# First projections and table products of the self attention issued in the last step of the cross attention, and the first step's queries rotated by VectorE

## The reference, cut to what matters

```python
x = x + tanh(g_xattn[0]) * _L0_xattn_ref(_layernorm(x), ctx_2048, ...)
x = x + tanh(g_ffn[0]) * _L0_ffn_ref(_layernorm(x), ...)
...
# inside _L0_ffn_ref: _attention(_layernorm(hidden_states, ln1_w, ln1_b), ...)
q = (h @ wq + bq); k = (h @ wk + bk); v = (h @ wv + bv)
q = q * cos + _rotate_half(q) * sin
k = k * cos + _rotate_half(k) * sin
scores = einsum('bhqd,bhkd->bhqk', q, k) / sqrt(HD)      # causal softmax
out = einsum('bhqk,bhkd->bhqd', probs, v) @ wo + bo
```

## Time and profile before

| what | value |
|---|---|
| median of 3 runs | 1759.58 us (1757.66 to 1762.4) |
| profiled execution, its own time | 1763.62 us |
| its span | 1761.7 us |
| mean granted TensorE clock | 0.978 |
| TensorE matmuls busy | 1665.8 us (95%) |
| VectorE busy | 1179.1 us (67%) |
| ScalarE busy | 1304.5 us (74%) |
| GpSimd busy | 1133.9 us (64%) |

### The profile page before, as it was taken

The page is one execution under the profiler, slowest core; times in us unless marked ns, Lnnn a source line. Parts: engine busy times, 40 slices in busy tenths (PEclk is TensorE's granted clock), DMA queues, the critical chain, the costliest instruction groups (busy, mean ns, idle before and its releaser), DMA issues.

```text
span 1761.7 us, 35497 instructions
## 1 busy us (share of the span) xinstructions
PE 1665.8 (95%) x11136; PEld 1513.4 (86%) x11136; DVE 1179.1 (67%) x3193; ACT 1304.5 (74%) x4205; POOL 1133.9 (64%) x1293
## 2 busy tenths in 40 slices
PE   6899998799999999999997996999999999999898
PEld 3788887688999999999996885899999999988897
DVE  5567668577775666566776787777777777776322
ACT  5677777598888888887874554898898988988321
POOL 5455536899998989898962214565655656676454
PEclk8899999899999999999998999999999999999998
DMA  4111211100000000000002010000000000000000
GB/s 148 51 40 36 67 32 55 43 19 13 19 19 13 15 24 13 20 13 20 13 7 93 23 30 8 13 9 12 10 12 13 9 13 16 17 15 15 10 19 25
DMA packets 32841, 45.87 MB, mean 26 GB/s; under 512 B 5264, under 2 KB 21904, under 8 KB 32656
## 3 DMA queue, kind: packets, MB, share of 16 engines
q1 hardware_dynamic: 32656, 43.59, 8.2%
HBM read 39.39 MB, written 4.19 MB: 25 GB/s over the span
## 4 chain that ended last, share of the span: by engine, by line
PE 75%; POOL 9%; DVE 7%; ACT 4%; issue 3%; DMA 1%; SPq 0%; POOLq 0%; DVEq 0%; ACTq 0%
PE pA L293 5%; PE pA L295 5%; PE pA L294 5%; PE pS L1112 4%; PE pF L293 4%; PE pF L295 4%; PE pF L294 4%; PE pS L1801 3%; PE pA L626 3%; PE pA L627 3%; PE pA L628 3%; PE pO L1131 3%; PE pF L827 3%; PE pT L1809 3%; PE pO L293 2%
## 5 line engine op out<-in xcount | busy, mean ns | idle before, releaser
L293 PE MATMUL pA<-Wh,XTh 128*128 128x512 f32 (+1 forms) x512 | 220.4, 430 | 7.4 <-SPq L119 3.8
L1533 POOL TENSOR_TENSOR f_sw<-f_sw,f_sin 128x512 f32<-128x512 f32 x128 | 181.8, 1420 | 34.6 <-ACT f_sw L1242 34.6
L295 PE MATMUL pA<-Wh,XTl 128*128 128x512 f32 (+1 forms) x512 | 188.7, 369 | 0.0
L294 PE MATMUL pA<-Wl,XTh 128*128 128x512 f32 (+1 forms) x512 | 188.4, 368 | 0.0
L1242 ACT ACTIVATE f_sw<-pA 64x512 f32<-64x512 f32 x256 | 151.5, 592 | 34.9 <-PE pA L628 31.1
L1536 POOL TENSOR_TENSOR f_sw<-f_sw,f_RB 128x512 f32<-128x512 f32 x128 | 169.5, 1324 | 10.0
L626 PE MATMUL pA<-XTh,Wh 128*128 128x256 f32 x512 | 163.8, 320 | 5.3 <-DVE f_qT L1385 5.3
L1914 ACT ACTIVATE x_P<-x_P,x_nm 128x192 f32<-128x192 f32 (+1 forms) x256 | 127.8, 504 | 49.9 <-DVE x_nm L1995 49.9
L1743 POOL TENSOR_TENSOR x_QR<-x_QR,x_t 128x512 f32<-128x512 f32 x64 | 82.2, 1284 | 103.5 <-DVE x_QR L1708 103.5
L628 PE MATMUL pA<-XTh,Wl 128*128 128x256 f32 x512 | 145.9, 285 | 0.0
L627 PE MATMUL pA<-XTl,Wh 128*128 128x256 f32 x512 | 145.8, 285 | 0.0
(11 more groups left out here) (317 smaller groups left out, 6278.8 us busy)
## 6 DMA issues: line engine op xcount, KB each, us to landing
RAW<-in_w_f SPq DMA_DIRECT2D x32, 256.0 KB, 2.6
RAW<-in_w_x SPq DMA_DIRECT2D x32, 192.0 KB, 2.4
RAW<-in_w_x SPq DMA_DIRECT2D x32, 160.0 KB, 2.3
x_base<-in_w_x0b SPq DMA_DIRECT2D x20, 192.0 KB, 2.5
RAW<-in_w_ff SPq DMA_DIRECT2D x8, 288.0 KB, 2.7
R<-in_x SPq DMA_DIRECT2D x4, 512.0 KB, 7.4
x_spill<-R SPq DMA_DIRECT2D x8, 256.0 KB, 2.0
RAW<-in_w_moe SPq DMA_DIRECT2D x8, 256.0 KB, 2.6
```

Source lines behind the costliest of these rows:

```text
L293: e.matmul(o, ah, bh, start=first, stop=False)
L294: e.matmul(o, ah, bl, start=False, stop=False)
L295: return e.matmul(o, al, bh, start=False, stop=last)
L1533: e.tensor_tensor(y, y, bc(sind[:, :], 1, 2), ALU.mult).then_inc(q["swm"], 1)
```

## The change

- TensorE: the first two projections (`next_proj(0)` and `(1)`) are issued ahead of `turn(31, 2)` and the output product of step 30; the third one (queries, n = 2) is issued behind the output product of step 31, ahead of `phase_end`, once VectorE has read the first.
- ScalarE: the tables RB for n = 0 and 1 and the exchanged copy of projection 0 go ahead of the exponentials of step 31, and the exchanged copy of projection 1 goes ahead of `phase_end`.
- VectorE: the output of step 30 is added ahead of the statistics; `take(0, 0)` goes in between; it makes the low parts of batches 2 and 3, which GpSimd made before.
- Step 0 of the self attention: the queries (n = 0 and 2) are rotated by VectorE (`rotate_first`, the three instructions that GpSimd had), the keys (n = 1 and 3) by GpSimd as before. The semaphore `rope` counts GpSimd's rotations alone, so each count on it is two less, and `rope0` counts VectorE's.
- RB is placed behind V in SBUF, so that the tables made early lie clear of the cross attention's tiles; `sw` and `rb` become semaphores that last over the phases.

```diff
@@ cross attention, pool / pe / act / dve @@
-                    if i in (29, 31):
-                        for b in (i - 29, i - 28):
+                    if i == 29:
+                        for b in (0, 1):
                             first_low(e, b, xa[b % 2])
...
+                    if last:
+                        next_proj(0)
+                        next_proj(1)
                     if i in (29, 31):
                         turn(i, i - 29)
...
                     else:
                         out_proj(i - 1, 1 - s)
-                        next_proj(0)
-                        next_proj(1)
...
                 out_proj(NI - 1, (NI - 1) % 2)
+                e.wait_ge(f0_q["taken"], 1)
+                self_proj_qk(e, 0, 2)
                 phase_end(e, name)
...
+                    if last:
+                        e.wait_ge(f0_q["const"], 96)
+                        e.wait_ge(q["sc"], 28)
+                        e.wait_ge(q["ap"], UNITS)
+                        e.wait_ge(q["split"], 28)
+                        f0_ahead["swapped_bias"](e, 0, 0)
+                        f0_ahead["swapped_bias"](e, 0, 1)
+                        f0_ahead["swapped"](e, 0, 0)
                     exp(i)
...
                 in_order(e, NI, body, 24)
+                f0_ahead["swapped"](e, 0, 1)
                 phase_end(e, name)
...
                     softmax(i, s)
+                    if last:
+                        add_out(i - 1)
                     if i >= 26:
                         e.wait_ge(q["acc"], i - 1)
                         first_stats(e, i - 26)
...
                     if last:
-                        for x in (i - 1, i):
-                            add_out(x)
-                            e.wait_ge(q["acc"], x + 1)
-                            first_stats(e, x - 24)
+                        e.wait_ge(f0_q["const"], 96)
+                        e.wait_ge(q["ap"], UNITS)
+                        f0_ahead["take"](e, 0, 0)
+                        e.wait_ge(q["acc"], i)
+                        first_stats(e, i - 25)
+                        add_out(i)
+                        e.wait_ge(n1["hi"], 4)
+                        first_low(e, 2, xa[0])
+                        first_low(e, 3, xa[1])
+                        e.wait_ge(q["acc"], i + 1)
+                        first_stats(e, i - 24)
@@ self attention, pe / act / dve / pool @@
                 def scores(i, h):
-                    e.wait_ge(q["rope"], NT * i + 2 * (h // 2) + 2)
+                    if i:
+                        e.wait_ge(q["rope"], NT * i + 2 * (h // 2))
+                    else:
+                        e.wait_ge(q["rope0"], h // 2 + 1)
+                        e.wait_ge(q["rope"], h // 2 + 1)
...
-                for n in range(2, NQ):
+                for n in range(3, NQ):
                     proj(0, n)
...
-                for n in range(NT):
+                for n in (2, 3):
+                    swapped(0, n)
                     swapped_bias(0, n)
-                    swapped(0, n)
...
+                def rotate_first(n):
+
+                    y, x = sw[:, n, :, :], qT[:, 0, n:n + 2, :]
+                    e.wait_ge(q["sw"], n + 1)
+                    e.tensor_tensor(y, y, bc(sind[:, :], 1, 2), ALU.mult).then_inc(q["swm0"], 1)
+                    e.wait_ge(q["swm0"], n // 2 + 1)
+                    e.wait_ge(q["rb"], 2 * n + 2)
+                    e.tensor_tensor(y, y, RB[:, 0, 2 * n:2 * n + 2, :], ALU.add).then_inc(q["swb0"], 1)
+                    e.wait_ge(q["swb0"], n // 2 + 1)
+                    e.wait_ge(q["taken"], n + 1)
+                    e.tensor_tensor(x, x, y, ALU.add).then_inc(q["rope0"], 1)
+
+                take(0, 1)
+                rotate_first(0)
+                take(0, 2)
+                take(0, 3)
+                take(0, 4)
+                rotate_first(2)
+                take(0, 5)
                 soft(0, 0)
...
                 for i in range(NI):
-                    for n in range(NT):
+                    for n in range(NT) if i else (1, 3):
                         rotate(i, n)
```

More of the change, by code:

```diff
@@ L165, in build @@
         ff_us = sb("ff_us", [P, FM])
-        f0_q = {x: lasting_sem("f0_" + x) for x in ("const", "bias0", "proj", "taken")}
+        f0_q = {x: lasting_sem("f0_" + x) for x in ("const", "bias0", "proj", "taken", "sw", "rb")}
+        f0_ahead = {}
         moe_q = {x: lasting_sem("moe_" + x) for x in ("up", "hlo")}
@@ L1038, in self_attention @@
             cosd, sind, mask, bqk, bv, bo = f0_tiles
-            RB = sb(name + "_RB", [P, 2, 2 * NT, S], F32, scope)
             sw = sb(name + "_sw", [P, NT, 2, S], F32, scope)
@@ L1073, in at_p, with swapped_part, swapped_bias_part, taken_part @@
                 return place["p", i, h]
+            def swapped_part(e, i, n):
+                m = NT * i + n
+                e.wait_ge(q["proj"], NQ * i + n + 1)
+                if i == 1 and n % 2 == 0:
+                    e.wait_ge(q["rope0"], n // 2 + 1)
+                elif i == 1:
+                    e.wait_ge(q["rope"], n // 2 + 1)
+                elif i:
+                    e.wait_ge(q["rope"], m - NT - 1)
+                for r in range(2):
+                    src, dst = slice(r * H2, (r + 1) * H2), slice((1 - r) * H2, (2 - r) * H2)
+                    ins = e.activation(sw[dst, n, :, :], pA[src, n % 2, :].rearrange("p (a n) -> p a n", a=2),
+                                       ACT.Copy)
+                ins.then_inc(q["sw"], 1)
+            def swapped_bias_part(e, g, n):
+                e.wait_ge(q["rope"], pos(NT * 8 * (g - 1) - 2))
+                for a in range(2):
+                    h = g * HG + 2 * (n // 2) + a
+                    e.activation(RB[:, g % 2, 2 * n + a, :], sind[:, :], ACT.Copy,
+                                 scale=bqk[:, 2 + n % 2, h:h + 1]).then_inc(q["rb"], 1)
+            def taken_part(e, i, n):
+                if n < 4:
+                    e.wait_ge(q["sw"], NT * i + n + 1)
+                    e.wait_ge(q["sc"], pos(HG * (i - 1)))
+                    x = (kT if n % 2 else qT)[:, i % 2, 2 * (n // 2):2 * (n // 2) + 2, :]
+                    for a in range(2):
+                        h = (i // 8) * HG + 2 * (n // 2) + a
+                        ins = e.scalar_tensor_tensor(x[:, a, :], pA[:, n % 2, a * S:(a + 1) * S],
+                                                     bqk[:, n % 2, h:h + 1], cosd[:, :], ALU.add, ALU.mult)
+                    ins.then_inc(q["taken"], 1)
+                else:
+                    g = i // 8
+                    e.wait_ge(q["proj"], NQ * i + n + 1)
+                    e.wait_ge(bias_in[g % 2], 16 * (g // 2 + 1))
+                    e.wait_ge(q["pv"], pos(HG * (i - 1)))
+                    e.tensor_tensor(V[:, i % 2, n - 4, :], pA[:, n % 2, :], bv[:, g % 2, :], ALU.add
+                                    ).then_inc(q["taken"], 1)
+            f0_ahead.update(swapped=swapped_part, swapped_bias=swapped_bias_part, take=taken_part)
             def sp(e):
@@ L1236, in swapped @@
                 def swapped(i, n):
[L1237 to L1251 removed]
+                    swapped_part(e, i, n)
+                def swapped_bias(g, n):
+                    swapped_bias_part(e, g, n)
                 def p_ev(i, h):
@@ L1378, in take @@
                 def take(i, n):
[L1379 to L1394 removed]
+                    taken_part(e, i, n)
                 def soft(i, h):
@@ L1449, in norm_rows @@
                     else:
-                        e.wait_ge(q["rope"], NT * 8 * (G - 1))
+                        e.wait_ge(q["rope"], NT * 8 * (G - 1) - 2)
                     norm.rows(e, b)
@@ L1456, in norm_low @@
                                     ALU.subtract).then_inc(q["nlo"], 1)
-                for n in range(NQ):
-                    take(0, n)
+                def rotate_first(n):
[15 more added lines that the diff above has]
+                take(0, 5)
                 soft(0, 0)
```

39 lines of the change are left out of this document (7 added, 32 removed).

## The result

The changed kernel takes 1751.6 us (median, 1748.84 to 1755.44) against 1761.36 us for the kernel before in the same comparison (1757.66 to 1762.76). The medians differ by 9.8 us; the ratio is 0.9948 with a 95% interval of 0.9935 to 0.9961, and by it the changed kernel is 9.2 us faster, between 6.9 and 11.4. The profiled execution took 1748.84 us, at a mean clock of 0.983.

What follows compares the result with a forecast made beforehand. GpSimd was taken to bound the first self-attention steps, now just ahead of TensorE, now just behind; 2.0 us (step 0 with the earlier seam) plus 4.8 (GpSimd's lead) gave 6.8, from 1759.58 to 1752.8 us, range 1747.5 to 1757.0.

Steps and rivals of the forecast that it cites:

- rival 1: Step 0: VectorE's rotations do not collide with GpSimd; total gain 10.8 us, 1748.8 us; chance 0.22 for gains of 8.5 up.
- Where TensorE's gain must come from: TensorE's holes between 312 and some 460 us: 3.57 and 5.29 around the seam, 1.35 and 2.50 waiting for GpSimd.
- Part 1, the seam: End of the cross attention: the seam comes 2.4 us earlier, bounds 0.9 and 2.7, with VectorE's list as the chain.
- rival 3: The seam does not come earlier (low parts behind the lock, VectorE's longer list); total gain 5.3 or 4; chance 0.12.
- Part 2, step 0: Self attention's step 0: 2.0 us earlier including the seam, despite VectorE's second rotation colliding with GpSimd; bounds 6 and 0.
- GpSimd's start 2.5 behind the seam: Step 0: GpSimd first clears 31 semaphores, taking 2.5 us, so VectorE's first query rotation escapes the collision.
- Part 3, GpSimd's lead: First self-attention steps: GpSimd, two rotations shorter, gets ahead and closes TensorE's waits; 4.8 us, bounds 1.4 and 5.3.
- rival 2: GpSimd's lead is not won, being fed late and newly colliding; total gain 2 to 3.4, 1757 us; chance 0.12.
- residue of 0.45: TensorE's second wait for GpSimd, 2.50 us long before, would keep 0.45 us, as copies feed GpSimd late.
- Rival 4: Slower: the clock stays at 1.2 GHz between and behind the seam's hole and the new one, reaching 1765; chance 0.03.

Runs made afterwards that it cites:

- e3: Changed kernel with the low parts of batches 2 and 3 made by GpSimd again, behind the coefficients of batch 5; ratio to the kernel before 0.9953.
- e4: Changed kernel with GpSimd's two key rotations of self-attention step 0 left out, so those keys stay unrotated; one run, 1745.81 us.
- e8: Changed kernel with a finished phase's semaphores cleared by SyncE instead of GpSimd, at every seam; ratio to the kernel before 0.9965.
- e2: Kernel before, with only VectorE's rotation of the step 0 queries added and everything at the seam as before; ratio to the kernel before 0.9984.
- e1: Changed kernel with the step 0 queries rotated by GpSimd again, early projections, tables and earlier seam kept; ratio to the kernel before 0.998.
- e5: Changed kernel with TensorE computing projection 2 of step 0 a second time ahead of the seam, filling part of the hole; one run, 1749.01 us.
- e11: Changed kernel with only VectorE's step 0 list reordered: both query rotations split and interleaved with takings and score scaling; ratio to the kernel before 0.9935.
- e12: The same program as e11, run once more in five rounds; ratio to the kernel before 0.9937.
- e7: Changed kernel with one more projection of step 0 (projection 3), a taking and a copy moved ahead of the seam; ratio to the kernel before 0.9957.

## Why the prediction was right, and where its sizes were off

The forecast was 1752.8, the time is 1751.6. The gain, 9.2 by time and 9.6 in the trace, is larger than the 6.8 forecast, and outside of the 5.3 to 8.5 that I had given half of the chance. That the time is off by only 1.2 is luck: the kernel before runs at 1761.3 to 1762.0 in the comparisons and I had subtracted from 1759.58, an error of 1.8 or more that nearly cancels the other. The size of the gain is that of rival 1 (8.5 and up, given 0.22), its mechanism (no collision) is not what happened.

1. **Where TensorE's gain must come from**: held. The holes of 3.57, 5.29, 1.35 and 2.50 were the ones that moved.
2. **Part 1, the seam**: forecast 2.4, measured 24.7 - 21.5 = 3.2 (so rival 3, no earlier seam, did not happen). The chain was the right one (VectorE's list, ended by its last statistics). VectorE's list begins where I had it (318.19 here, 320.2 with the 2.0 of drift) and takes 6.2 us, where I had added durations to 7.0. Its instructions start before the one ahead has ended: the two low parts, 0.68 each, stand 0.60 apart (322.18, 322.78). Nor did they wait for GpSimd. So 3.2, above my bound of 2.7: a sum of such a list goes by the starts. e3 shows the other side: left on GpSimd, they make the seam 1.3 later.
3. **Part 2, step 0**: forecast 2.0 with the seam, measured 5.1. The terms: the seam 0.8; the projection behind the first scores at T+12.9 instead of T+13.5, 0.6; 1.5 for a low clock behind its hole, which did not come, since the hole was 0.97 and not 3.5; and 0.2 of arithmetic, as 3.3 less 1.5 is 1.8 and not the 2.0 of the prediction (some 0.2 stays unexplained). The collision was there, but in another pattern. I had the first rotation free and three collisions in the second, to end it at T+12.8; one fell in the first (1.69) and two in the second, which ended at T+12.3. Its price was nearly right: 0.69 becomes 1.65 to 1.69, where I had said near 1.9, when GpSimd is just into an instruction, and it stays 0.68 or 0.69 throughout where GpSimd has only copies of one column to do (e4). The Trainium skill (SBUF — State Buffer, "SBUF: two separate sides") says that of a VectorE instruction with two SBUF inputs and a GpSimd one that reads SBUF the one that starts first has the shared ports for its whole instruction, and the other waits. The trace agrees: VectorE's third instruction began at 326.95, 0.12 behind one of GpSimd's that ended at 328.10, and took 1.69.
4. **GpSimd's start 2.5 behind the seam**: 2.4. e8 shows that it is the clearing, and that it keeps GpSimd out of two of the first rotation's instructions. It shows too that this shield is worth little: without it the first rotation collides three times, and with GpSimd's earlier start set against that, the stretch is 0.3 longer. What the sum leaned on without my seeing it is that the two parts need each other: the rotation alone (e2) loses 1.7 in step 0, the seam alone (e1) waits 4.0 there for GpSimd.
5. **Part 3, GpSimd's lead**: forecast 4.8, measured 9.6 - 5.1 = 4.5, and 4.5 by itself in e2 (so rival 2 did not happen). Both waits are gone and the window of 0.64 with them: 1.1 us at the first, for which I had 1.35, and 3.3 at the second with the clock behind it, for which I had 3.45. My residue of 0.45 isn't there: that GpSimd is fed late shows on GpSimd (1.61 at 337.03), not on TensorE.
6. **Rival 4**, a clock that stays low: no. It was back to 1.00 from 336 us on. e5, and e11 beside e12, show that what it takes before that is slack.

The step that failed most was part 2's: a hole of 3.5 us before the projection behind the first scores, and 1.5 us of low clock behind it. The runs show a hole of 0.97 and no low clock there. Second is the seam, 0.8 too small. The wider error is to price every hole of TensorE at the low clock's cost. Between 325 and 337 us TensorE is not the chain: VectorE's list is, as e5, e7 and e11 show.

## What to carry to other kernels

When the instructions of two engines hold each other up, look less at how many collide than at what stands behind each in its engine's list; splitting a helper and putting the collisions where less waits for them gave 1.4 us with more of them. A gain of an edit can hang on another edit: measure halves, and where they don't add up, look in each half for the wait that the other half removes. In these runs a low clock cost nothing where TensorE waited for VectorE anyway; check by what the next hole does.

## What I had not expected of the hardware

- **The same hole, another clock.** Behind the hole of 3.05 us the window from 328 us has 0.50 in the changed kernel, 0.59 in e12 and 1.00 in e11 and in e8 (where it falls in the next window, to 0.59); e11 and e12 are one program. So the trace of one execution does not say what the clock does behind a hole of this length in the next one.
- **It is a large part of the drift between two profiles.** At the second cross attention's first products and at the last ones, the same matmuls in the changed kernel and in e7 (rows of 8 us, after, then e7):

```profile
1088.00:1096.00 8.00, 7.01 (x34) 6.04 (x35) 4.19 (x13) 3.79 (x12) 5.07 (x10) 0.81 0.01 2
1736.00:1744.00 8.00, 4.49 (x36) 4.29 (x36) 0.69 (x1) 0.00 (x0) 2.57 (x4) 1.00 0.11 35
```

```profile
1091.00:1099.00 8.00, 7.29 (x24) 6.13 (x25) 3.27 (x11) 2.94 (x8) 5.04 (x10) 0.50 0.00 0
1742.00:1750.00 8.00, 6.60 (x34) 6.61 (x35) 0.00 (x0) 0.00 (x0) 1.26 (x3) 0.57 0.11 35
```

  Each place costs e7's profile some 2.6 us more, and both programs are the same there. Its span is 8.1 us longer: 1.1 in the stretch, 1.8 ahead of it, and these two.
- **Clearing a semaphore on GpSimd costs some 0.07 us** (an estimate: 31 of them 2.3 us, from e8), and the engine is not shown as busy in that time.
